# A graph kernel on one core: pairs of edges spread in rows by TensorE, x loaded in parts, a pipelined product with w0

## The reference

```
deg = max(number of edges that end in a node, 1)
h   = relu(layernorm(x))
x1  = x + relu(deg^-1/2 * segment_sum((deg^-1/2 * (h @ w0))[src], dst) + bias0)
h   = relu(layernorm(x1))
for each of 2 layers:
    q, k, v = projections of h, 8 heads of 64
    scores of each edge; softmax over the edges that end in a node; weighted sum of v; @ Wo; batch norm
    relu(@ W1) @ W2; batch norm
out = x1 + layernorm(...)
```

## Time and profile before

| | |
|---|---|
| median of 3 runs | 3433.01 us |
| the 3 runs | 3420.39, 3433.01, 3434.41 us |
| the profiled execution: its time | 3420.37 us |
| its span (what the profile shows) | 3418.6 us, so 1.8 us lie around it |
| mean granted clock of TensorE | 0.969 of full speed |
| zeros issued / POOL's first indirect DMA / its last | 4.1 / 73.0 / 908.0 us |
| product with w0, first and last instruction on ACT | 130.6 / 272.0 us |
| first and last merge of the tile loop | 291.3 / 922.2 us |
| attention starts | 987.8 us |

### The profile page before, as it was taken

How to read it: one execution, slowest core, us unless ns; L and a number is a source line. 1 busy time by engine, 2 the same in 40 slices (tenths; PEclk the granted TensorE clock), 3 DMA queues, 4 the chain that set the end, 5 groups by cost and what they waited for, 6 DMA issues and landing times. The chain is left out here.

```text
span 3418.6 us, 72329 instructions
## 1 busy us (share of the span) xinstructions
PE 3044.7 (89%) x24802; PEld 2394.4 (70%) x24802; DVE 2269.7 (66%) x6951; ACT 1953.9 (57%) x3918; POOL 2156.7 (63%) x1979
## 2 busy tenths in 40 slices
PE   2367999998769999999999989989999999999985
PEld 2123656654448888888888877767888888888874
DVE  8694344432237888888888853237888888888856
ACT  0123444443337778777777721227778778777734
POOL 1687888887527777777777710017777777777734
PEclk9998999998889999999999999999999999999998
DMA  9656666654479999999999821239999999889951
GB/s 372 99 129 139 122 133 117 125 104 90 111 181 175 165 170 169 166 166 175 165 163 165 152 74 31 54 72 175 168 165 168 168 171 170 166 163 168 158 122 60
DMA packets 1297433, 496.25 MB, mean 145 GB/s; under 512 B 1237211, under 2 KB 1262836, under 8 KB 1291379
## 3 DMA queue, kind: packets, MB, share of 16 engines
q1 hardware_dynamic: 1156168, 459.71, 67.3%
q0 software_dynamic: 133120, 0.80, 4.0%
q10 hardware_dynamic: 7788, 31.21, 2.8%
HBM read 153.04 MB, written 79.96 MB: 68 GB/s over the span
## 5 line engine op out<-in xcount | busy, mean ns | idle before, releaser
L1422 DVE CUSTOM_DVE_ANT_0 prob<-s_ps,mask 125x500 f32<-125x500 f32 x1600 | 1057.9, 673 | 286.0 <-PE s_ps L1267 207.9
L1199 POOL TENSOR_TENSOR staged<-prob,staged 125x500 f16<-125x500 f32 x960 | 1065.8, 1116 | 156.8 <-ACT staged L1193 94.7
L1359 ACT ACTIVATE prob<-prob,neg_max 125x1000 f32<-125x1000 f32 (+1 forms) x960 | 954.6, 994 | 114.5 <-DVE scrap L1428 112.8
L1267 PE MATMUL s_ps<-keys,queries 128*125 128x500 f16 x3200 | 945.7, 378 | 41.4 <-DMA queries<-q_tiles 29.2
L500 POOL DMA_INDIRECT counts<-count,cell x320 | 657.5, 2055 | 245.7 <-issue 107.5
L1300 PEld LDWEIGHTS o_ps<-values,across 125*125 125x125 f16 x7680 | 591.3, 138 | 200.5 <-issue 58.2
L1300 PE MATMUL o_ps<-values,across 125*125 125x128 f16 x7680 | 607.0, 222 | 38.2 <-DMA across<-staged 37.6
L1193 POOL CAST staged<-prob 125x500 f16<-125x500 f32 x640 | 385.6, 602 | 376.0 <-ACT prob L1359 252.8
L1435 DVE TENSOR_TENSOR p_lo<-t_ps,p_hi 125x500 f16<-125x500 f32 x640 | 432.0, 675 | 91.1 <-ACT p_hi L1369 90.8
L1278 PE MATMUL t_ps<-identity,prob 125*125 125x125 f32 x2560 | 412.5, 284 | 2.5 <-ACT agg L1379 2.2
L1369 ACT CAST p_hi<-t_ps 125x500 f16<-125x500 f32 x640 | 361.2, 564 | 85.9 <-PE t_ps L1278 85.6
(11 more groups left out here) (152 smaller groups left out, 3499.3 us busy)
## 6 DMA issues: line engine op xcount, KB each, us to landing
mask<-bias_rows SPq DMA_DIRECT2D x200, 218.8 KB
counts<-xt ACTq DMA_DIRECT2D x8, 3054.0 KB, 37.2
keys<-counts SPq DMA_DIRECT2D x40, 546.9 KB
bias_rows<-edge_bias SPq DMA_DIRECT2D x20, 1093.8 KB
queries<-q_tiles SPq DMA_DIRECT2D x80, 250.0 KB, 3.8
pair_row<-pair_flat SPq DMA_DIRECT2D x40, 437.5 KB
across<-staged SPq DMA_TRANSPOSE x960, 3.3
q_tiles<-q_both SPq DMA_DIRECT2D x80, 125.0 KB, 2.7
```

Source lines behind the costliest of these rows:

```text
L1199: engine.tensor_tensor(here[0:P, BPC:2 * BPC, 0:P], prob[u % PROBS][:, k * KC:(k + 1) * KC].rearrange("p (s c) -> p s c", s=BPC), here[0:P ...
L1267: mm = pe.matmul(s_ps[n % SB][:, 0:KC], lhsT=queries[b][:, h, part, :], rhs=keys[:, h, c * KC:(c + 1) * KC], start=(part == 0), stop=(part ...
L1359: act.activation(here, here, ACT.Exp, bias=neg_max[u % 4][:, :], accum_out=sums[u // H % 2][:, u % H, piece:piece + 1]).then_inc(exped, 1)
L1422: dve.tensor_tensor_reduce(out=prob[u % PROBS][:, at], in0=s_ps[n % SB][:, 0:KC], in1=bias[b][:, at], scale=1.0, scalar=MASKED, op0=ALU.ad ...
```

## The change

Five things change in `front`:

1. **Rows of pairs by PE.** `pair_run`, `pair_flat` and `pair_row` are gone, and the second layout of the edges with them. PE transposes a column of `pair`, repeated 125 times with a step of 0, into PSUM: four columns (two groups, a "row") fill one bank, two banks (`v_ps`, `x1_ps`) take turns, 80 rows in all (`spread_row`). DVE's tallies read that bank instead of SBUF. A row waits until the row two before it has been tallied. The short instructions that end a block now stand between tallies of the next block.
2. **x in parts.** ACT waits until the zeros have landed, then loads x in four parts of five tiles, at most two at a time, then w0. DVE takes each part's statistics with a block of tallies between parts. Ten blocks stand ahead of the statistics instead of five, fourteen ahead of the first h.
3. **The product with w0 in a pipeline.** ACT and PE work on tile t+1's norm, transpose and copy before tile t's product is read; PE spreads two or three rows of pairs after each product.
4. **Needed groups from each column's least node.** PE transposes dst once, DVE takes minima over 125 edges, PE spreads them over 20 partitions, DVE does one comparison over 320 columns and one reduction.
5. **Smaller things.** The degrees go to DRAM and back on SP's queue, early, not on ACT's queue behind x. The one-hots are laid out the other way round, with the ramp written out in full (2560 elements, made on POOL) and the columns innermost.

The core of the diff:

```diff
-    pair_flat = dram("pair_flat", [1, E], F32)
+        row_ps, dst_ps = (v_ps, x1_ps), agg_ps[0]
@@ SP @@
-                load_rows(sp, dst_run_i[:, :], dst_runs, runs_loaded)
-                load_rows(sp, src_run_i[:, :], src_runs, runs_loaded)
...
-                for k in range(NB):
-                    if k >= 2:
-                        sp.wait_ge(rows_used, k - 1)
-                    at = slice(k * PER_ROW * GE, (k + 1) * PER_ROW * GE)
-                    load_rows(sp, pair_row[k % 2][:, :], pair_flat[:, at].broadcast_to([EP, PER_ROW * GE]), rows_loaded[k % 2])
+                sp.wait_ge(deg_ready, 1)
+                sp.dma_start(deg_flat.rearrange("(a b) o -> a (b o)", b=LO), deg_sb[:, :]).then_inc(deg_stored, 16)
+                sp.wait_ge(deg_stored, 16)
+                sp.dma_start(deg_col[:, :], deg_flat[0:N, :].rearrange("(t p) o -> p (t o)", p=P),
@@ POOL @@
+                pool.iota(ramp_i[:, :, :], pattern=[[1, LO], [0, QC]], base=0, channel_multiplier=0).then_inc(ramps_ready, 1)
+                pool.wait_ge(ramps_ready, 1)
+                pool.tensor_copy(ramp[:, :, :], ramp_i[:, :, :]).then_inc(ramps_ready, 1)
@@ DVE @@
+                def tally_column(at):
+                    row, own = at // RC, (at % RC) // GC
+                    if at % RC == 0:
+                        dve.wait_ge(rows_turned, row + 1)
+                    if at >= 2:
+                        dve.wait_ge(tallied, at - 1)
+                    after = GE - EP - (at % GC) * EP
+                    dve.scalar_tensor_tensor(
+                        matches[at % 2][:, :], row_ps[row % 2][0:EP, own * GE:(own + 1) * GE], pair[:, at:at + 1],
+                        earlier[:, after:after + GE], ALU.is_equal, ALU.mult, accum_out=tally[:, at:at + 1]).then_inc(tallied, 1)
...
+                    for c in range(BC):
+                        tally_column(k * BC + c)
+                        if c == 2 and k >= 1:
+                            count_block(k - 1)
+                        if c == 4 and k >= 1:
+                            place_block(k - 1)
...
+                for k in range(EARLY + 2, AHEAD):
                     tallies(k)
-                dve.wait_ge(x_loaded, BOTH)
-                for t in range(NT):
-                    steps.done(dve.bn_stats(stats[:, t, :], x_sb[:, t, :]))
+                for part in range(XPARTS):
+                    x_statistics(part)
+                    if part + 1 < XPARTS:
+                        tallies(AHEAD + part)
@@ ACT @@
-                load_rows(act, x_sb[:, :, :], x.rearrange("(t p) d -> p t d", p=P), x_loaded)
+                act.wait_ge(zeroed, 16 * ZDMAS)
+                for part in range(XPARTS):
+                    if part >= 2:
+                        act.wait_ge(x_loaded[part % 2], BOTH * (part // 2))
+                    tiles = slice(part * XT, (part + 1) * XT)
+                    load_rows(act, x_sb[:, tiles, :], x.rearrange("(t p) d -> p t d", p=P)[:, tiles, :], x_loaded[part % 2])
...
+                first_norm(0)
+                first_norm(1)
+                keep_ht(0)
+                for t in range(NT):
+                    if t + 1 < NT:
+                        keep_ht(t + 1)
+                    if t + 2 < NT:
+                        first_norm(t + 2)
+                    keep_hw(t)
@@ PE @@
+                def spread_row(n):
+                    if n >= 2:
+                        pe.wait_ge(tallied, RC * (n - 1))
+                    for c in range(RC):
+                        mm = pe.transpose(row_ps[n % 2][0:EP, c * EP:(c + 1) * EP],
+                                          pair[:, n * RC + c:n * RC + c + 1].broadcast_to([EP, EP]), identity[0:EP, 0:EP])
+                    mm.then_inc(rows_turned, 1)
...
+                turn_h(0)
+                for t in range(NT):
+                    if t + 1 < NT:
+                        turn_h(t + 1)
+                    times_w0(t)
+                    for n in range(done + (NROW - done) * t // NT, done + (NROW - done) * (t + 1) // NT):
+                        spread_row(n)
```

More of the change, by code:

```diff
@@ L245, in front @@
             group_i = sb(first, "group_i", [EP, NCOL], I32)
-            src_run_i = sb(first, "src_run_i", [EP, NCOL], I32)
-            dst_run_i = sb(first, "dst_run_i", [EP, NCOL], I32)
-            pair_run = sb(first, "pair_run", [EP, NCOL])
-            pair_row = [sb(first, f"pair_row{b}", [EP, PER_ROW * GE]) for b in range(2)]
             matches = [sb(first, f"matches{r}", [EP, GE], BF16) for r in range(2)]
@@ L508, in _, with count_block @@
                 steps = Steps(dve, dve_steps)
-                def tallies(k):
-                    dve.wait_ge(rows_loaded[k % 2], BOTH * (k // 2 + 1))
-                    for c in range(BC):
-                        if c >= 2:
-                            steps.wait(but=1)
-                        own = slice((c // GC) * GE, (c // GC + 1) * GE)
-                        after = GE - EP - (c % GC) * EP
-                        at = k * BC + c
-                        steps.done(dve.scalar_tensor_tensor(
-                            matches[c % 2][:, :], pair_row[k % 2][:, own], pair[:, at:at + 1],
-                            earlier[:, after:after + GE], ALU.is_equal, ALU.mult, accum_out=tally[:, at:at + 1]))
-                    steps.wait()
-                    dve.sem_inc(rows_used, 1)
+                def tally_column(at):
[8 more added lines that the diff above has]
+                        earlier[:, after:after + GE], ALU.is_equal, ALU.mult, accum_out=tally[:, at:at + 1]).then_inc(tallied, 1)
+                def count_block(k):
                     at = slice(k * BC, (k + 1) * BC)
+                    dve.wait_ge(tallied, (k + 1) * BC)
+                    if k >= 1:
+                        dve.wait_ge(cells_ready, k)
                     steps.done(dve.scalar_tensor_tensor(moved[:, :], tally[:, at], LATER - 0.5, to_spare[:, at],
@@ new lines, in tallies, with x_statistics @@
+                def tallies(k):
+                    for c in range(BC):
[4 more added lines that the diff above has]
+                            place_block(k - 1)
+                def x_statistics(part):
+                    dve.wait_ge(x_loaded[part % 2], BOTH * (part // 2 + 1))
+                    for t in range(part * XT, (part + 1) * XT):
+                        steps.done(dve.bn_stats(stats[:, t, :], x_sb[:, t, :]))
@@ new lines, in _ @@
+                steps.wait()
+                dve.sem_inc(needed_ready, 1)
+                tallies(EARLY)
+                dve.wait_ge(needed_turned, 2)
+                steps.done(dve.scalar_tensor_tensor(below[:, :], needed_ps[:, 0:NCOL], tile_end[:, :], group_i[0:NT, :],
+                                                    ALU.is_lt, ALU.mult))
+                steps.wait()
+                steps.done(dve.tensor_reduce(needed_col[:, :], below[:, :], AXX, ALU.max))
+                steps.wait()
@@ L805, in _ @@
             def _(pe):
+                def spread_row(n):
[5 more added lines that the diff above has]
+                    mm.then_inc(rows_turned, 1)
+                pe.wait_ge(consts_ready, 3)
+                pe.wait_ge(pairs_ready, 2)
+                spread_row(0)
+                spread_row(1)
+                for c in range(3):
+                    columns = slice(128 * c, min(128 * (c + 1), NCOL))
+                    mm = pe.transpose(dst_ps[0:columns.stop - columns.start, c * EP:(c + 1) * EP], dst[:, columns], identity[0:EP, 0:EP])
+                mm.then_inc(needed_turned, 1)
                 for q in range(QP):
```

165 lines of the change are left out of this document (84 added, 81 removed).

## The result

The changed kernel takes 3445.8 us (median of 6 runs, 3435.4 to 3449.8) against 3424.6 (3414.7 to 3434.4): a ratio of **1.0063**, 95% interval 1.0045 to 1.0080. It is slower by 0.6%, where 3427 us and no change were forecast. As a difference, -5.7 us were forecast and +21.2 measured: the 3427 went by the median of three runs, 3433.0, which with three more runs is 3424.6. Executions in a slower state (6436 and 9501 us, where they occurred) are left out of every ratio. The profiled execution took 3449.8 us, its span is 3447.9.

The account below looks back on a forecast made before the run. The prediction took POOL's chain of 320 indirect DMAs to end the first stage; its terms, -3.7 - 5 - 3 + 6 = -5.7 us, against the median of 3433.01 gave 3427 us, no change, range 3407 to 3441.

Parts of the forecast that it names:

- the change touches only the first 990 us: Opening step: only the first stage is affected, so the question is which wait ends that stage.
- the tail: End of the first stage, from the last tile's load to attention's start: 76 us that nothing in the change touches.
- Zeros: Start of POOL's chain: zeros land earlier as less data fills the DMA engines; -3.7 us, bounds -6 and -2.
- Early waits: POOL's first groups, waiting for DMAs to land while x and w0 load: -5 us, between 0 and -20.7.
- POOL's instructions: POOL's indirect DMAs beside DVE's tallies, 130 to 270 us, get shorter: -3 us, between 0 and -6.
- Waiting tiles: Tile loop: 1.7 more tiles wait for POOL, each costing 3.4 us; +6 us, between +3 and +8.
- Pipeline: Pipelined product with w0: first merge 25 us earlier, at 258 to 276, only lengthening PE's wait for POOL; worth 0.
- B: Rival: the earlier product carries through, the first stage's end follows PE, 25 us earlier; 3408 us, chance 0.05.
- C: Rival: POOL gains and no tile joins the waiting ones; -12 us, 3421 us, chance 0.12.
- D: Rival: TensorE at 1.2 GHz in the product with w0, first merge 55 us late; +14, 3447 us, chance 0.08.
- E: Rival: DVE's tallies from PSUM are slow, delaying the first merge; +61 us at 8 us a block, in D's chance.
- A: Rival: POOL runs free, early waits go entirely (-20.7); -23 us in all, 3410 us, chance 0.21.

Follow-up runs that it names:

- a_room: Changed kernel with pair_flat's 160,000 bytes declared in DRAM again, unused, so later DRAM tensors lie at their old addresses; ratio 1.0057 to the kernel before.
- a_sems: Changed kernel with two unused semaphores allocated first, so later stages have the semaphore numbers of the kernel before; 2462.5 us behind the first load of queries.
- a_again: The changed kernel run once more, nothing altered; 2464.4 us behind the first load of queries, 49.5 us a tile.
- a_one: Changed kernel with 59 short transposes more on TensorE, and x loaded in one part instead of four; 3404.4 us beside 3420.6 (one execution).
- a_rows: a_p59 with SP also loading 40 blocks of broadcast rows for nobody, as much traffic as the old rows; scatter's last DMA at 910.2 us.
- a_p59: Changed kernel with 59 short 8x8 transposes more on TensorE, once, ahead of the first tile of the counts; ratio 0.9946 to the kernel before.

## Why the prediction was wrong

**The step that failed** is the first paragraph's: "the change touches only the first 990 us". Sum, rivals and range had no term for the 2430.8 us behind the first load of queries. They grew by 39.4 us in the profiled execution, 29 to 34 in its repeats (a_room, a_sems, a_again), since 325 matmuls more on TensorE moved its fetches by half a packet against the transposes. The prediction counted these matmuls by their time and their place beside POOL, not by their number. It was to be seen beforehand: the page has the queue q8, and the programs give the number. What the place would be worth was not, without a run at another place.

**The first stage** was right in its mechanism and too small in size. POOL's chain still bounds it, and the tail is 74.9 us (76.0 before). But its end came 10.1 us earlier (13 to 14 in the repeats) where 5.7 were forecast. By its terms:

- *Zeros, -3.7*: -5.9, at the edge of its bounds; POOL starts at 67.10 instead of 72.96.
- *Early waits, -5*: -8.1; seventh DMA 26.5 us behind the first instead of 34.6. By a_one some 4.7 of it are the parts of x, for which I had taken 0 by the volume. By the rule of the Trainium skill cited there ("DMA: Bandwidth & Descriptors", section "Queues, rings and completion order") cutting x would not help; the measurement decides, and it is against this here: 30.0 us in one part, 25.3 in four.
- *POOL's instructions, -3*: from 130 to 250 us the mean fell from 2074 to 1974 ns, to where it is undisturbed, so -5. That is the value that the rule of the Trainium skill gave ("SBUF — State Buffer", section "SBUF: two separate sides": GpSimd shares a port pair with VectorE while VectorE reads two inputs from SBUF), and a_rows supports it by ruling out the traffic. Over all 320 instructions it is -11.8; the part after the end of the tallies, in the tile loop, stays unexplained.
- *Waiting tiles, +6*: POOL's pauses above 1 us behind its seventh DMA sum to 84.6 us instead of 66.2, +18 (+13 to +18 in a_again, a_room and a_p59). Tile 12's load, 40.3 us behind the one before, is the first that stands apart; tile 13's was before. This term was the most undersized.
- *Pipeline, 0*: the first merge came at 261.0, between 258 and 276, and moved nothing. On the way two durations were off: the ramp's iota took 2.5 us and not 9.0, and the degree matmuls, which now read with a stride, took 319 ns instead of 242, so that DVE waited 18.0 us for PE in the one-hots. That the stride is the reason is inferred from the two layouts.

**The rivals.** B, C, D and E did not occur: SP still waits 117.7 us for POOL from 700 to 915, and the clock from 130 to 270 us was 0.90. With the fetches put back (a_p59), the whole came to 3402.2 us against 3418.3, -16, and in its profile all of that is the first stage (971.0 against 987.8). That is between the forecast's -5.7 and A's -23, nearer to A, but not by A's mechanism: in a_p59 the early waits gave 9.3 us of the 20.7 that A wanted.

## What to carry to other kernels

When a change adds or takes instructions on an engine that is the bound in a later, DMA-filled loop, ask where its instruction fetches will stand in that loop: compare the packets of the instruction queue with the loop's period, and if they are nearly locked (here 4.02 a tile), expect a per cent either way from code that nobody touched. Before judging such a change, pad the stream to the old phase, or try three or four paddings of both kernels; the padding alone was worth more here than the change. And a difference that sits in untouched stages and comes again (here 29 to 39 us in four executions) is no noise: divide the span at a landmark first, then compare addresses, numbers and streams of the two programs.

## What the runs showed of the hardware

- DRAM-to-DRAM copies beside the transposes of SP's queue: two packets of 16,384 bytes, four times a tile, on engines 93% busy with transposes cost 1.2 to 1.4 us a tile of 48.6; two of 64 bytes cost 0.1 to 0.4. Sixteen of 4 bytes cost 1.2 to 1.6, sixteen of 1,024 bytes 0.3 to 0.4.
- The cost of a fetch by its place is no smooth curve. Over the tiles of ten traces, from a layer's third tile on, a tile takes a mean of 48.2 to 48.4 us when its first fetch starts 4 to 6 us into it (55 tiles), and 50.1 when it starts 1 to 2 us into it (33 tiles).
- A contiguous copy of one row was cut into 16 packets at 16,384 bytes and at 64; two rows that don't join stayed two packets at both sizes.
- A transpose by DMA lands 0.8 us later (4.19 instead of 3.43) when a packet of instructions starts close to its issue in the changed kernel, 0.45 us later (3.90 instead of 3.45) in the kernel before.
- A matmul of 125x64 with one-hots read at a stride took 319 ns, 242 with dense ones.
